# P's 512-column tiles with two buffers, AV one slot later, x normalised in place, two buffers shared

## The reference, cut to what matters

```python
xn = layernorm(x)
qkv = xn @ w_qkv.T + b_qkv                      # 16 heads of 32
scores = q @ k.T / sqrt(32) + causal mask       # per head, 512 x 512
attn = softmax(scores)
a = (attn @ v) @ w_out.T + b_out
g, u = (xn @ gate_w.T) * gate_s, (xn @ up_w.T) * up_s      # 1408 columns
f = ((silu(g) * u) @ down_w.T) * down_s
out = x + a + f
```

## Time and profile before

| | us |
|---|---|
| median of 3 runs | 1947.92 (1947.15 to 1948.87) |
| the profiled execution | 1948.99, its span 1947.2 |
| TensorE busy | 1866.0 (96%) |
| VectorE busy | 1504.4 (77%) |
| ACT busy | 1450.8 (75%) |
| GpSimd busy | 1255.8 (64%) |

### The profile page before, as it was taken

How to read it: one execution, slowest core, us unless ns; L and a number is a source line. 1 busy time by engine, 2 the same in 40 slices (tenths; PEclk the granted TensorE clock), 3 DMA queues, 4 the chain that set the end, 5 groups by cost and what they waited for, 6 DMA issues and landing times.

```text
span 1947.2 us, 44190 instructions
## 1 busy us (share of the span) xinstructions
PE 1866.0 (96%) x14978; PEld 1222.0 (63%) x14978; DVE 1504.4 (77%) x4516; ACT 1450.8 (75%) x4280; POOL 1255.8 (64%) x1800
## 2 busy tenths in 40 slices
PE   6689999999999999999999999999999999999997
PEld 4456566665766666566666756666566666756663
DVE  4677778777787877878778787877878777787884
ACT  4677687867778787787877778777787777777683
POOL 4676666857577585776857576575666656576462
PEclk9899999999999999999999999999999999999998
DMA  7997978889798796978889798786968878797674
GB/s 217 216 171 141 185 134 182 159 151 184 134 191 144 159 182 127 205 139 170 166 144 193 136 178 138 156 168 122 198 129 169 144 142 175 135 187 129 122 157 94
DMA packets 818839, 310.26 MB, mean 159 GB/s; under 512 B 756464, under 2 KB 789232, under 8 KB 818608
## 3 DMA queue, kind: packets, MB, share of 16 engines
q1 hardware_dynamic: 800928, 249.44, 70.9%
q0 software_dynamic: 17680, 57.95, 10.4%
HBM read 55.59 MB, written 16.78 MB: 37 GB/s over the span
## 4 chain that ended last, share of the span: by engine, by line
PE 70%; DVE 9%; DMA 6%; SPq 6%; ACT 5%; issue 3%; POOL 2%; POOLq 0%; ACTq 0%; DVEq 0%
PE bank L287 70%; DMA pt<-phl 5%; SPq L947 4%; DVE phl L598 3%; ACT phl L492 2%; DVE bank L588 1%; SPq L954 1%; ACT bank L500 1%; DVE res L625 1%; DVE small L562 1%; DVE xhl L737 1%; ACT small L488 0%; SPq L939 0%; DMA xnT<-in_up_dram 0%; DVE ft L608 0%
## 5 line engine op out<-in xcount | busy, mean ns | idle before, releaser
L598 DVE SCALAR_TENSOR_TENSOR phl<-bank,small,phl 128x512 f16<-128x512 f32 (+3 forms) x1024 | 526.6, 546 | 187.9 <-ACT phl L492 184.9
L500 ACT ACTIVATE bank<-bank,small 128x512 f32<-128x512 f32 (+3 forms) x1024 | 516.0, 505 | 167.2 <-DVE small L588 166.4
L588 DVE CUSTOM_DVE_ANT_0 bank<-bank,mask 128x512 f32<-128x512 f32 (+3 forms) x1024 | 484.3, 504 | 162.8 <-PE bank L287 160.4
L492 ACT ACTIVATE phl<-bank,small 128x512 f16<-128x512 f32 (+3 forms) x1024 | 500.0, 531 | 91.6 <-DMA pt<-phl 81.0
L287 PE MATMUL bank<-xnT,wg 128*128 128x256 f16 x2816 | 367.8, 273 | 6.5 <-DVE fh L613 4.8
L287 PE MATMUL bank<-xnT,wu 128*128 128x256 f16 x2816 | 367.4, 274 | 0.0
L287 PE MATMUL bank<-xnT,wqkv 128*128 128x512 f16 x1536 | 352.4, 379 | 1.1 <-ACT q L461 1.1
L287 PE MATMUL bank<-wd,ht 128*128 128x512 f16 x1408 | 317.5, 381 | 4.0 <-POOL ht L810 2.1
L287 PEld LDWEIGHTS bank<-xnT,wg 128*128 128x128 f16 x2816 | 264.0, 98 | 68.9 <-issue 5.9
L287 PEld LDWEIGHTS bank<-xnT,wu 128*128 128x128 f16 x2816 | 276.6, 98 | 33.0
L287 PE MATMUL bank<-stk 96*128 96x512 f16 (+3 forms) x1024 | 245.8, 301 | 26.6 <-DVE phl L598 25.2
(11 more groups left out here) (110 smaller groups left out, 2195.6 us busy)
## 6 DMA issues: line engine op xcount, KB each, us to landing
stk<-qkp SPq DMA_DIRECT2D x768, 64.0 KB, 2.1
res<-in_x_dram POOLq DMA_DIRECT2D x64, 256.0 KB, 4.7
xin<-in_x_dram POOLq DMA_DIRECT2D x60, 256.0 KB, 4.6
out_dram<-res POOLq DMA_DIRECT2D x60, 256.0 KB, 3.7
pt<-phl SPq DMA_TRANSPOSE x512, 4.2
xin<-in_gate_dram POOLq DMA_DIRECT2D x11, 256.0 KB, 3.5
xin<-in_up_dram POOLq DMA_DIRECT2D x11, 256.0 KB, 3.3
xin<-in_down_dram POOLq DMA_DIRECT2D x11, 256.0 KB, 3.5
```

The costliest lines, as they stand in the source:

```text
L492: i = eng.activation(phl[qt][:, j % 2, 0], pb[:, off:off + W], ACT.Copy, scale=st_r[:, c:c + 1])
L500: i = eng.activation(pb[:, off:off + W], pb[:, off:off + W], ACT.Exp, bias=st_m[:, c:c + 1], scale=-1.0, accum_out=st_s[:, c:c + 1])
L588: i = eng.tensor_tensor_reduce(out=bk[:, off:off + W], in0=bk[:, off:off + W], in1=mask[:, 512 - W:512], scale=-(32.0 ** -0.5) / (QS * QS) ...
L598: i = eng.scalar_tensor_tensor(phl[qt][:, j % 2, 1], pb[:, off:off + W], st_r[:, c:c + 1], phl[qt][:, j % 2, 0], ALU.mult, ALU.subtract)
```

## The change

P's 512-column tile, `phl[3]`, becomes two buffers, one for each pair of heads, each with its own semaphore `d_pt[3][p]`; the shorter widths keep one buffer. AV moves from slot 4 to slot 5 of the next group, except for the last group. The transposition of heads 0 and 1 at 512 columns is issued by SP in slot 6 instead of 5. x is normalised within `xin` and `xs32` is gone; since `xin` is then held for longer, the loads of x are issued one slot later, except the first ones. `dtmp`, in which the scaled down result lies, is now `q32[0]`, in which ACT drains AV; new waits keep the two users apart, and the weight conversion ends its use of it at slot 15.

```diff
-    phl = [sb(f"phl{i}", [128, 2, 2, 128 * (i + 1)], F16) for i in range(4)]
+    phl = [[sb(f"phl{i}", [128, 2, 2, 128 * (i + 1)], F16)] for i in range(3)]
+    phl.append([sb(f"phl3_{p}", [128, 2, 2, 512], F16) for p in range(2)])
...
-    dtmp = sb("dtmp", [128, 512], F32)
+    dtmp = q32[0]
...
-    xs32 = sb("xs32", [128, 512], F32)
...
-    d_pt = [sem(f"d_pt{i}") for i in range(4)]
+    d_pt = [[sem(f"d_pt{i}")] for i in range(3)] + [[sem(f"d_pt3_{p}") for p in range(2)]]
...
-    AV_K, QK_K = 4, (3, 6)
+    AV_K, QK_K = 5, (3, 6)
...
-    av_at = {U * (G + 1) + AV_K: G for G in range(NGRP)}
+    av_at = {U * (G + 1) + (AV_K if G < NGRP - 1 else 4): G for G in range(NGRP)}
+
+    avs_ahead = {bt: sum(n < m for n in av_at) for m, bt in d_at.items()}
+    ds_ahead = {G: sum(n < m for n in d_at) for m, G in av_at.items()}
...
-    later = [(n - 4, ("norm", *v)) for n, v in norm_at.items()] + [(n - 3, ("check", c)) for n, c in check_at.items()]
+    later = [(n - (4 if n < 4 else 3), ("norm", *v)) for n, v in norm_at.items()] + [(n - 3, ("check", c)) for n, c in check_at.items()]
...
-        xin_reader[i] = {"norm": (v_xs, 4 * what[1] + what[-1] + 1), "check": (a_ms, what[1] + 1), "wout": (v_wo, what[1] + 1)}[what[0]]
+        xin_reader[i] = {"norm": (v_xl, 4 * what[1] + what[-1] + 1), "check": (a_ms, what[1] + 1), "wout": (v_wo, what[1] + 1)}[what[0]]
...
-    stage += [(x0[2], 15), (x0[3], 20), (dtmp[:, :], 20)]
+    stage += [(x0[2], 15), (x0[3], 20), (dtmp[:, :], 15)]
+    part = lambda qt, j: phl[qt][j // 2 if qt == 3 else 0]
...
         def drain_av(G):
             g = G % 4
+            if G == 0:
+                w.wait_ge(*finished[slot_last[14]])
             w.wait_ge(p_al, G)
+            w.wait_ge(p_dy, ds_ahead[G])
...
             for j, qt, off in segs(u):
-                w.wait_ge(d_pt[qt], 16 * (2 * G + j // 2))
+                w.wait_ge(*((d_pt[3][j // 2], 16 * G) if qt == 3 else (d_pt[qt][0], 16 * (2 * G + j // 2))))
...
-        def scaled(i, t, xs, xi):
+        def scaled(i, t, xi):
             st = lst[t]
-            w.wait_ge(v_xl, i if i > 4 else 0)
             w.wait_ge(p_rs, i + 1)
-            eng.tensor_scalar(xs, xi, st[:, 6:7], st[:, 8:9], op0=ALU.subtract, op1=ALU.mult).then_inc(v_xs, 1)
+            eng.tensor_scalar(xi, xi, st[:, 6:7], st[:, 8:9], op0=ALU.subtract, op1=ALU.mult).then_inc(v_xs, 1)
...
         def down_scale(b, t):
             w.wait_ge(p_set, 9)
-            w.wait_ge(*finished[slot_last[14]])
             w.wait_ge(p_dy, 4 * b + t)
+            w.wait_ge(p_al, avs_ahead[b, t])
...
-                if k == 5:
-                    turn_p(G, 0, 3, n - 4)
                 if k == 6:
+                    turn_p(G, 0, 3, n - 5)
                     turn_p(G, 0, 2, n - 3)
                     turn_p(G, 0, 0, n - 3)
```

More of the change, by code:

```diff
@@ L329, in av @@
             b, g = divmod(G, 4)
-            for qt in range(4):
-                w.wait_ge(d_pt[qt], 16 * (2 * G + 2))
+            for qt in range(3):
+                w.wait_ge(d_pt[qt][0], 16 * (2 * G + 2))
+            for p in range(2):
+                w.wait_ge(d_pt[3][p], 16 * (G + 1))
             w.wait_ge(v_vl, 4 * b + 2 * (g // 2) + 2)
@@ L491, in high @@
                 c, W = 2 * (n % NSTAT) + k, 128 * (qt + 1)
-                i = eng.activation(phl[qt][:, j % 2, 0], pb[:, off:off + W], ACT.Copy, scale=st_r[:, c:c + 1])
+                i = eng.activation(part(qt, j)[:, j % 2, 0], pb[:, off:off + W], ACT.Copy, scale=st_r[:, c:c + 1])
             i.then_inc(a_hi, 1)
@@ L504, in scalar_program @@
         for t in range(4):
-            hl = xhl[t][:, 0] if t < 2 else phl[3][:, t - 2, 0]
+            hl = xhl[t][:, 0] if t < 2 else phl[3][0][:, t - 2, 0]
             w.wait_ge(v_xs, t + 1)
@@ L597, in low @@
                 c, W = 2 * (n % NSTAT) + k, 128 * (qt + 1)
-                i = eng.scalar_tensor_tensor(phl[qt][:, j % 2, 1], pb[:, off:off + W], st_r[:, c:c + 1], phl[qt][:, j % 2, 0],
+                i = eng.scalar_tensor_tensor(part(qt, j)[:, j % 2, 1], pb[:, off:off + W], st_r[:, c:c + 1], part(qt, j)[:, j % 2, 0],
                                              ALU.mult, ALU.subtract)
@@ L616, in v_low @@
             psum = job_bank["v", b, hf, tp][:, :].rearrange("p (a f) -> p a f", a=2)
-            part = lambda p: vv[:, p, 2 * tp:2 * tp + 2, 256 * hf:256 * hf + 256]
+            half_of = lambda p: vv[:, p, 2 * tp:2 * tp + 2, 256 * hf:256 * hf + 256]
             w.wait_ge(a_vh, 4 * b + 2 * hf + tp + 1)
-            eng.scalar_tensor_tensor(part(1), psum, QS / (XS * WS), part(0), ALU.mult, ALU.subtract).then_inc(v_vl, 1)
+            eng.scalar_tensor_tensor(half_of(1), psum, QS / (XS * WS), half_of(0), ALU.mult, ALU.subtract).then_inc(v_vl, 1)
         def out_add(b, t):
@@ L687, in first_low @@
         def first_low(t):
-            hl = xhl[t][:, :, :] if t < 2 else phl[3][:, t - 2]
+            hl = xhl[t][:, :, :] if t < 2 else phl[3][0][:, t - 2]
             w.wait_ge(a_xh, t + 1)
@@ L736, in vector_program @@
                 w.wait_ge(p_xh, 4 * b + t - 3)
-                eng.tensor_tensor(hl[:, 1], xs32[:, :], hl[:, 0], ALU.subtract).then_inc(v_xl, 1)
+                w.wait_ge(v_xs, 4 * b + t + 1)
+                eng.tensor_tensor(hl[:, 1], xin[t % 2][:, :], hl[:, 0], ALU.subtract).then_inc(v_xl, 1)
             if n - 2 in norm_at:
                 b, t = norm_at[n - 2]
-                scaled(4 * b + t, t, xs32[:, :], xin[t % 2][:, :])
+                scaled(4 * b + t, t, xin[t % 2][:, :])
             if n - 1 in wout_at:
@@ L907, in gpsimd_program @@
                 w.wait_ge(v_xs, i + 1)
-                eng.tensor_scalar(xhl[t % 2][:, 0], xs32[:, :], 1.0, 1.0, op0=ALU.mult, op1=ALU.mult).then_inc(p_xh, 1)
+                eng.tensor_scalar(xhl[t % 2][:, 0], xin[t % 2][:, :], 1.0, 1.0, op0=ALU.mult, op1=ALU.mult).then_inc(p_xh, 1)
             for i in range(W_FIRST, NCH):
@@ L954, in turn_p @@
             eng.dma_start_transpose(pt[p][:, 12 * qt:12 * qt + nb, :],
-                                    phl[qt][:, :, :, :].rearrange("p a b c -> p (a b c)")).then_inc(d_pt[qt], 16)
+                                    part(qt, 2 * p)[:, :, :, :].rearrange("p a b c -> p (a b c)")).then_inc(d_pt[qt][p if qt == 3 else 0], 16)
         for t in range(4):
@@ L964, in sync_program @@
         for t in range(4):
-            turn_x(0, t, xhl[t] if t < 2 else phl[3][:, t - 2])
+            turn_x(0, t, xhl[t] if t < 2 else phl[3][0][:, t - 2])
             load_weight(4 + t)
```

## The result

The changed kernel takes 1971.43 us (median of 4 runs, 1970.13 to 1974.98) against 1947.54 us for the kernel before on the same chip (4 runs). The ratio is 1.0115 with a 95% interval of 1.0095 to 1.0136: **1.2% slower, some 22 us**. The forecast was 1948.8 with a range of 1934 to 1960. The profiled execution has a span of 1969.0 us, 21.8 more than before.

A forecast was written before the change was run, and what follows sets the result against it. TensorE, busy 1866.0 of 1947.2 us, was taken as the bound. The terms 24.2 - 14.0 - 5.5 - 0.8 - 3.0 = +0.9 us, on the median of 1947.92, gave 1948.8, with a range of 1934 to 1960.

The forecast's parts named there:

- second tile, net of POOL's wait: Waits for low before unit 9 and for POOL's hidden tile, 16.4 + 2.1, go; 4.5 stays at slot 19: 14.0 us less.
- x in place, shared buffers: Normalising x in its own tile and sharing dtmp and a stage entry: put at nothing.
- issue waits before AV: TensorE's waits before AV for its last transposed tile are all shorter than the 1.9 us moved ahead: 5.5 us less.
- start: First stage: AV starts when it did, only what follows is shortened, up to the first down product: 0.8 us less.
- output products wait for the split: Slot 7, groups with G%4 = 0: products wait for POOL's AV split, 1.65 us in 14 batches, 1.05 in the last: 24.2 more.
- cover of gate/up (4) and scores (5): Slots 4 and 5: gate/up and scores come ahead of AV, 1.9 us of work; no wait of theirs was forecast.
- end: Last stage: ACT's 1.5 us transposition wait goes and AV(62) fills TensorE's wait for low: 3.0 us less, bounds 1.5 and 5.
- the first sentence on AV: Slots 4 and 5: TensorE has the same work in another order, gate/up and scores (1.9 us) ahead of AV.
- The lock rival: POOL's split beside VectorE's normalisation and subtraction loses 0.55 us on the shared ports: 7.7 more, 1956.5; chance 0.08.
- The case without the wait: Output products don't meet POOL's split, TensorE later or drain earlier: the 24.2 go, 1924.6; chance 0.12.
- Double-buffering: The skill's rule, taken alone, would let the change gain all 22.0 us of TensorE's waits.
- The slower rival: Group 4b+1, POOL's slot 6: a late drain makes POOL idle and the down product wait: 1962.8; chance 0.12.

The follow-up runs named there:

- run 1: The changed kernel with AV back in slot 4, all else of the change kept: 1938.98 us, 0.9933 of the kernel before.
- run 12: The changed kernel with AV in slot 4, one 512-column tile, and its transposition issued in slot 5 as before: 1951.34 us, 1.0013 of the kernel before.
- run 9: Also av5_outp: the changed kernel with AV at slot 5 only for each batch's last group, slot 4 elsewhere: 1958.77 us, 1.0062 of the kernel before.
- run 10: The changed kernel with AV at slot 5 in three groups, slot 4 in each batch's last group: 1954.21 us, 1.0032 of the kernel before.
- run 3: Also xload4: the changed kernel with all loads of x issued four slots ahead again: 1961.87 us, 1.0056 of the kernel before.
- run 4: The changed kernel with AV ahead of the scores within slot 5: 1973.51 us, 1.0119 of the kernel before.
- run 11: The changed kernel with AV in slot 4, POOL's residual additions one slot later and x loads at n - 4: 1955.75 us, 1.0032 of the kernel before.

## Why the prediction was wrong

**By its terms.** Waits are from the profiles, times in us:

| step | predicted | measured |
|---|---|---|
| second tile, net of POOL's wait | -14.0 | -16, from -10 to -21 (run 1 against run 12); in the waits 16.4 + 2.1 gone, 1.0 left |
| x in place, shared buffers | 0 | 0.0013 of the time, not told from none |
| issue waits before AV | -5.5 | -5.5 (7.2 to 1.7) |
| start | -0.8 | -1.6, the first down product at 104.03 instead of 105.60 (below) |
| output products wait for the split | +24.2 | +27.7 in 14 waits; +25 in the time (run 9 against run 1) |
| cover of gate/up (4) and scores (5) | 0 | +14.5 (8.5 + 6.0); +19 in the time (run 10 against run 1) |
| granted clock, batches 2 to 14 | not in it | +3.4 |
| end | -3.0 | -4.1, but 1.0 only in the waits (below) |

**The step that failed** is the first sentence on AV: that in slots 4 and 5 "TensorE has the same work in another order". It looked at what AV waited for and at what waited for AV, and not at what AV had covered. AV was 1.8 us of work ahead of a gate product that needs VectorE's hidden product and of scores that need low(1), and the room behind it was 0.47 us in group 33, a number that was in the trace of before. VectorE's queue comes to low(1) only 0.4 us earlier, so TensorE waits when it comes 1.7 earlier. That is +14.5 us in the waits of the changed kernel, and run 10 has it alone: +19 us. For the loads of x the prediction names the work that hides them and what would stand without it; it never asked that of AV as a cover for others.

**The output products.** Place, cause and order of the wait were right, and its size nearly: 1.83 for 1.65. It was read from one batch, and the three batches with L654 in the way add 1.8 us. The drain began within 0.02 us of the forecast. The case without the wait is out. In the last batch the prediction had a wait of 1.05 that didn't come.

**The lock rival** came true in a smaller size. Beside L580, L802 took 1.40 in 13 of the 14 places and 1.21 in the other, where it takes 1.16 nearly everywhere else (1.48 in four places where nobody waits for it); run 3 moved it and had 1.15. The rival had put 0.55 on it. In run 3 the two meet in the other order: L802 had 1.04 us to go when L580 began, and L580 took 1.32 instead of 0.54, so it lost 0.78. The Trainium skill (SBUF — State Buffer, "SBUF: two separate sides") says that where a VectorE instruction that uses the shared pair of ports meets one of GpSimd, the later one stands until the first has ended. L580 had 0.39 us to go when L802 began in the changed kernel, and L802 lost 0.25. The meeting from which the prediction read its 0.55 is of the same kind: L737 began at 1008.79, and L782 had 0.69 us to go. So the direction agrees each time and the size is below it; that L580 is one of the instructions that use this pair is taken from these meetings.

**The clock.** The prediction took no account of what follows a wait. Around the end of two of the three waits of 2.4 us (those that end at 549.69 and 909.61) the granted clock fell from its upper to its lower level, 1.2 GHz, for a part of the stretch; behind the wait of 1.83 us in group 32 it didn't. Windows of the changed kernel of 5 us each, the columns as above, the granted clock third from the end:

```profile
550.50:555.50 5.00, 5.00 (x19) 2.02 (x17) 1.50 (x6) 1.32 (x3) 2.59 (x4) 0.66 0.67 121
909.00:914.00 5.00, 4.39 (x14) 1.69 (x15) 1.11 (x6) 1.92 (x7) 3.92 (x6) 0.66 0.94 193
1029.50:1034.50 5.00, 4.58 (x23) 2.16 (x24) 2.48 (x10) 2.57 (x9) 3.73 (x6) 1.00 0.98 209
```

As an estimate, 2 x 5.00 x (1 - 0.66) = 3.4 us. Of the 7.0 us that TensorE is busier in batches 2 to 14, the other 3.6 are not explained.

**The start and the end came out near their numbers, but not for the reasons given.** The prediction left the first AV where it was. It began 3.3 us earlier, before and then after:

```profile
87.82 3.39 PE L287 MATMUL bank<-pt,vv 128*32 128x512 f16 x48 [11.61 <-DMA pt<-phl]
```
```profile
84.56 3.39 PE L291 MATMUL bank<-pt,vv 128*32 128x512 f16 x48 [5.41 <-DMA pt<-phl]
```

Most of this was then lost again at the last weight, whose wait grew from 1.9 to 7.4 us. At the end the prediction had waits for `low` filled by AV(62). The two in question went from 2.4 to 2.6 us, and TensorE's idle time of the last batch fell by 1.0 us only. The rest of the 4.1 is busy time, at a higher granted clock. The last batch, before and then after:

```profile
1811.30:1947.30 136.00, 118.55 (x939) 73.82 (x937) 97.39 (x296) 86.12 (x256) 58.79 (x83) 0.94 0.64 125
```
```profile
1837.20:1969.10 131.90, 115.44 (x939) 73.15 (x937) 97.04 (x296) 86.36 (x256) 59.03 (x83) 0.97 0.67 129
```

The kernel before has two falls of the clock more there (0.66 over 1900 to 1905 us and over 1910 to 1915), so over the whole execution the clock costs the changed kernel nothing (mean granted clock 0.992, before 0.990). That both terms lie near what was measured is luck.

**The second tile.** The mechanism was right, and -14.0 lies within what the runs leave (-10 to -21). What is late next was right too: in run 1 POOL's hidden tile, 6.9 us in ten waits for the 4.5 assumed. In the changed kernel itself it is 1.0, and run 4 shows it come back as 9.6 when the scores are covered. That meeting was seen as a pair (unit 9 and the down product) and is a chain of three: low(1), low(5), the hidden tile.

**Double-buffering.** The rule of the Trainium skill (Trainium Kernel Development and Optimization, "Best Practices") to double-buffer for performance was weighed with a gain of up to 22.0 us. The second tile did give some 16 of them. What ate them was the order that came with it, AV behind the work that it had covered.

**The sum.** Middle batches: the prediction had +4.0 (13 x 1.65 - 16.4 - 2.1 + 4.5 - 3.5), the trace +28.4. In exactly these batches the waits for `low` were 13.3 us before (the other 3.1 of the 16.4 are one wait in batch 1), and 8.5 for `low` and 5.4 for the hidden product stand there after. Of the 24.4 between, the output wait has 25.7 - 21.4 = 4.3, the lost cover 13.9, the wait in batch 1 3.1, the clock 3.4, the unexplained busy time 3.6, and POOL's wait, 1.0 instead of 4.5, -3.5. That is 24.8. The range failed because it was built from the sizes of known terms and from rivals at the same two places. It had no case in which the moved work leaves something bare. The slower rival, the split of AV ahead of the down product, is not what happened: that product waits once, for 1.0 us.

## What to carry to other kernels

Work that is moved in an in-order queue is a cover for what stands behind it: for each instruction that it passes, read from the trace by how much its operands were ready before it began. Where that room is shorter than the moved work, the rest of it can turn into waiting. And a wait at one meeting hides the next one, so take a change apart by groups or slots on the chip before adding up its parts; here keeping all of the change but AV's slot, and moving POOL's residual additions instead, turns +1.2% into -0.9%.

## What was not expected of the hardware

- The fall of the granted clock does not follow from the length of the wait alone: two of three waits of 2.4 us had it, and in av5_outp it fell behind one of 1.95 us (to 0.66 over 5 us), while none came behind a wait of 3.12 us in the kernel before and one of 2.64 us in xload4. The row of av5_outp:

```profile
1611.50:1616.50 5.00, 4.48 (x14) 1.74 (x15) 1.02 (x4) 1.92 (x6) 3.82 (x6) 0.66 1.08 219
```

- A transposition's time to land is not steady: in run 11 the last one of a group 4b took 3.1 to 3.7 us in nine batches from the third on and 5.7 to 6.3 in four. Each of the four costs about 4 us of waiting, and in the one at 1031 us the granted clock was 0.50 over the next 5 us.
- POOL's root of the variance (L834, L825 in the kernel before, 128x1) takes either 0.57 us or 0.93 to 1.02. In the kernel before two of the four tiles of a batch are slow, in the changed kernel three, and with the loads of x at n - 4 again (runs 3 and 11) one, with the same operands. This is 7.7 of the 15.7 us that POOL is busier. Why the place of the load matters to it is open; no wait of TensorE in the steady part names it.
